# Four graph layers on one core: the last pass as a ring walk, the fronts moved ahead, a longer ring in the first attention pass

## The chip, the cores and the metric
One NeuronCore of one Trainium2 chip. The metric is device time in microseconds (us) of a whole run; the kernel before took 5873.08 us (median of 3 runs, 5872.82 to 5876.18).

## The reference, cut to what matters
A graph of 6250 nodes with 128 features and 100,000 edges, sorted by destination. Four layers, each on `h = relu(layernorm(x))`, each added to `x`:

```python
# layer 0: two GraphSAGE convolutions (mean of the sources' rows, two 128x128 products), elu, log_softmax
# layer 1: attention with 4 heads over the edges and a loop per node, batch norm, 128-512-128 feed-forward, batch norm
# layer 2: attention with 2 heads of 64, prelu
# layer 3:
for r in range(4):
    hr = x_src @ weight[r] + bias[r]          # x_src = h[src]
    msg = where(rel == r, hr, msg)
agg = segment_max(msg, dst); agg = 0 for nodes without edges
x = x + h @ weight[4] + bias[4] + agg
```

Destinations are 6250 u^2 with u uniform, so low nodes have most of the edges.

## The kernel before
Nodes lie as 49 tiles of 128 (NT), in 7 groups of 7 tiles (NG). Edges are padded to 100,352: 784 tiles of 128 (ET). `x` and `h` stay in SBUF. Every layer has a projection (`project`), which normalises the nodes of a group on VectorE and ScalarE (the front), transposes and multiplies on TensorE and writes a table to DRAM, and then a pass over the edges, in which GpSimd gathers the table's rows by edge, 128 rows an instruction.

**Walks.** The two GraphSAGE passes and the second attention pass walk a ring: GpSimd fills slots of 7 tiles (896 edges, GE; 112 groups, GN), and the other engines go through 160 steps (SN), one for each pair of a group and a block of 128 nodes that it touches, with 14 matmul instructions a step that select and add up by products with a one-hot matrix (`add_up`, L1194). `walk_steps` (L880) lays the body of a step out for each engine. The first attention pass does the same with groups of 512 edges, 196 of them in 248 steps, and a ring of QR = 17 groups at the start of `arena`.

**The last pass** is the only one left that doesn't walk. `edge_pass` (defined at L397, called at L2880) goes over 196 chunks of 512 edges. GpSimd gathers four tiles (L422) into one of four slots, with indices that ScalarE copied to `slot` (L514). TensorE transposes the chunk (L495), so that features lie on partitions and edges along them; VectorE scans it (L471): the running maximum, broken by a mask (`cut_row`, loaded by SP, L433) where the destination changes. TensorE transposes it back (L505), ScalarE copies it out of PSUM (L525) and stores all 512 rows to `scan_rows` in DRAM (L531). When all is stored, `gather_results` (L557) has GpSimd gather the row of each node's last edge, 49 times 128 rows, VectorE adds each group of seven to `x` (L2890), and SP stores `out`.

**Projections.** In `project` (L585) VectorE makes front(0) and front(1), then for each group i, where start rows are scattered, waits for the product, copies it (post) and makes front(i+2). GpSimd scatters each group's start rows by seven indirect DMAs (L620), behind the post. In the `by_tile` form TensorE multiplies tile by tile into four PSUM banks, with the transposes of the next group (L650) before tile 4; ScalarE copies the transposed group (L691) and each tile's product (L699). Posts are at L1501 (projection 1), L2405 (2) and L2871 (the y projection of the last layer, L2874).

The passes' starts in the trace: GraphSAGE 58 and 1080 us, first attention pass 2184, projection 2 3552, second attention pass 3664, y projection 4704, last pass 4816.

Of the kernel before, what the change touches and what calls it, by code (L numbers as in the profile page):

```python
# [8 lines left out]
I32 = mybir.dt.int32  # L9
# [4 lines left out]
P = 128  # L14
# [3 lines left out]
NG = 7  # L18
# [10 lines left out]
CHUNKS = ET // CT  # L29
ITERS = CHUNKS // NB  # L30
# [32 lines left out]
QR = 17  # L63
# [61 lines left out]
def build(nc, a, out):  # L125
    assert NT % NG == 0 and ET % CT == 0 and CHUNKS % NB == 0
    groups = NT // NG
    with ExitStack() as ctx:
# [19 lines left out]
        scan_rows = dram("scan_rows", [EP + P, D])  # L148
# [5 lines left out]
        x = sb("x", [P, NT, D])  # L154
        h = sb("h", [P, NT, D])
        arena = sb("arena", [P, 14336])
# [10 lines left out]
        block_col = sb("block_col", [P, 2])  # L167
        last_dst = sb("last_dst", [GN, 1], I32)
# [10 lines left out]
        y_idx = sb("y_idx", [P, ET + (NB + 1) * CT], I32)  # L179
        last_idx = sb("last_idx", [P, NT], I32)  # L180
        start_idx = sb("start_idx", [P, NT], I32)
        slot = sb("slot", [P, NB, CT], I32)
# [62 lines left out]
        group_rows = [count(f"group_rows{b}") for b in range(2)]  # L245
        group_here = count("group_here")
        own_loaded = [count(f"own_loaded{b}") for b in range(2)]
# [4 lines left out]
        gathered = [count(f"gathered{c}") for c in range(NB)]  # L252
        idx_staged = count("idx_staged")
        hot_made = [count(f"hot_made{a}", 2 * LQ) for a in range(2)]
        lo_apart = count("lo_apart")
        numbers_loaded = [count(f"numbers_loaded{b}") for b in range(2)]
        picked = count("picked", NB)
        summed = count("summed", NB)
        chunk_weighted = count("chunk_weighted")
# [18 lines left out]
        own_kept = count("own_kept")  # L278
        own_product = count("own_product")
# [40 lines left out]
        chunk_turned = count("chunk_turned", NB)  # L320
        chunk_scanned = count("chunk_scanned", NB)
        chunk_back = count("chunk_back", 2)
        chunk_copied = count("chunk_copied", 2)
        written = [count(f"written{b}", 16) for b in range(2)]
        mask_loaded = [count(f"mask_loaded{c}") for c in range(NB)]
# [62 lines left out]
        def laps(engine, first, body, n=NB, times=ITERS):  # L388

            first()  # L390
            with engine.Fori(0, times - 1) as i:
                for c in range(n):
                    body(i, c, True)
            for c in range(n):
                body(times - 1, c, c < n - 1)

        def edge_pass(table, width, idx, mask_row, op0, op1, mode="plain"):  # L397

            beside = H1 if mode == "heads" else 0
            target = scan1_rows if beside else scan_rows

            def written_rows(b):
                return out_rows[:, b, 0:CT * (D + beside)].rearrange("p (t d) -> p t d", d=D + beside)

            def rows(c, t):  # L410
                n = (c * CT + t) * width
                return arena[:, n:n + width]

            with nc.Block() as block:
                @block.gpsimd
                def _(pool):
                    with pool.Fori(0, ITERS) as i:
                        for c in range(NB):

                            wait_apart(pool, idx_staged.sem, idx_staged.past(i * NB + c + 1))  # L420
                            for t in range(CT):
# [3 lines left out]
                                ).then_inc(gathered[c].sem, 16)  # L425

                @block.sync
                def _(sp):
                    with sp.Fori(0, ITERS) as i:
                        for c in range(NB):  # L430
                            k = i * NB + c
# [2490 lines left out]
```

## Time and profile before

| | us |
|---|---|
| median of 3 runs | 5873.08 |
| the profiled execution | 5876.16 |
| its span | 5874.4 |
| TensorE matmul busy in it | 3278.1 (56%) |
| VectorE busy | 2906.4 (49%) |
| ScalarE busy | 1827.9 (31%) |
| GpSimd busy | 3903.4 (66%) |

Busy time of GpSimd is that of its gathers alone; the 0.3 us between two gathers isn't in it. A page line of the costliest groups gives the line of the kernel, engine, operation, tiles written and read, the count, then busy time, mean ns of one, and idle time of the engine just before them with what ended it.

### The profile page before, as it was taken

The page shows a single profiled execution, that of the slowest core. Times are in us where ns is not written, and L with a number is a line of the kernel's source. Part 1 is how long each engine was busy: PE and PEld are TensorE (multiplying, and loading weights), DVE is VectorE, ACT ScalarE, POOL GpSimd, SP SyncE. Part 2 cuts the span into 40 slices and gives each one's busy share as a digit, 9 for nine tenths or more (in the row PEclk, how much of TensorE's full clock was granted, in tenths as well). Part 3 has the DMA queues.
Part 4 walks back from the last instruction along what each step waited for, and adds up shares of the span by engine and source line. Part 5 has one row for each costly group of instructions (what it writes and reads, how often), then busy time and mean ns, then how long its engine had stood idle before and what let it go on. Part 6 is the DMA issues. An engine that isn't in the chain of part 4 may idle for free. (4 is left out here: it accounts for less than half of the span.)

```text
span 5874.4 us, 89970 instructions
## 1 busy us (share of the span) xinstructions
PE 3278.1 (56%) x15772; PEld 2756.8 (47%) x15773; DVE 2906.4 (49%) x7625; ACT 1827.9 (31%) x6493; POOL 3903.4 (66%) x4083
## 2 busy tenths in 40 slices
PE   3444555545555525889999894244555563334332
PEld 3444455444555523677777644233445533333331
DVE  4233344434455656788888852344555652222221
ACT  2111111111122213666666653233344441111110
POOL 4777777677777747777776003777777517777776
PEclk9667777766677756999999995566677785555555
DMA  4222222211111112344444211222222134444443
GB/s 122 61 62 63 63 65 66 72 53 52 53 53 52 53 41 78 111 113 117 119 117 113 95 46 31 52 53 54 53 53 52 38 111 130 133 132 130 131 133 107
DMA packets 441899, 474.71 MB, mean 81 GB/s; under 512 B 131954, under 2 KB 337214, under 8 KB 441695
## 3 DMA queue, kind: packets, MB, share of 16 engines
q0 software_dynamic: 130464, 264.37, 17.1%
q1 hardware_dynamic: 184116, 146.31, 8.3%
q10 hardware_dynamic: 127227, 63.09, 3.6%
q14 instruction: 69, 0.57, 0.0%
q8 instruction: 23, 0.38, 0.0%
HBM read 315.46 MB, written 157.97 MB: 81 GB/s over the span
## 5 line engine op out<-in xcount | busy, mean ns | idle before, releaser
L1194 PE MATMUL pa<-arena,weighted 128*128 x4480 | 860.0, 367 | 855.8 <-POOLq L913 511.2
L1194 PEld LDWEIGHTS pa<-arena,weighted 128*128 128x128 f32 x4480 | 795.4, 273 | 909.4 <-issue 909.2
L422 POOL DMA_INDIRECT arena<-y_tab,slot x784 | 739.8, 944 | 398.7 <-issue 209.4
L1607 POOL DMA_INDIRECT arena<-t_tab,src_idx x784 | 777.5, 992 | 265.7 <-issue 216.0
L919 POOL DMA_INDIRECT arena<-h_tab,src_idx x784 | 742.8, 947 | 308.1 <-issue 221.9
L2490 POOL DMA_INDIRECT arena<-t_tab,src_idx x784 | 753.3, 961 | 244.9 <-issue 224.6
L919 POOL DMA_INDIRECT arena<-sage_tab,src_idx x784 | 739.8, 944 | 262.4 <-issue 216.1
L471 DVE TENSOR_TENSOR_SCAN scan_t<-mask,scan_t,pa 128x512 f32<-128x512 bf16 x196 | 250.9, 1280 | 737.1 <-PE pa L495 737.1
L495 PE MATMUL pa<-ident,arena 128*128 128x128 f32 x784 | 218.3, 434 | 603.9 <-DMA arena<-y_tab,slot 603.9
L495 PEld LDWEIGHTS pa<-ident,arena 128*128 128x128 f32 x784 | 140.1, 217 | 681.9 <-DMA arena<-y_tab,slot 430.8
L2731 PE MATMUL pa<-weighted 128*128 128x130 f32 x2240 | 422.6, 364 | 21.0 <-ACT weighted L2809 11.0
L2731 PEld LDWEIGHTS pa<-weighted 128*128 128x128 f32 x2240 | 392.7, 271 | 34.4 <-issue 19.7
L620 POOL DMA_INDIRECT start_rows<-nodeval,start_idx x98 | 98.5, 1005 | 455.1 <-DVE nodeval L2405 372.6
L1056 DVE TENSOR_TENSOR weighted<-pd,rel 128x896 f32<-128x896 f32 x320 | 348.3, 1089 | 51.8 <-issue 47.2
L1064 DVE SCALAR_TENSOR_TENSOR scan_t<-scan_t,alpha,pa 128x130 f32<-128x130 f32 x320 | 110.5, 345 | 503.7 <-PE pb L1201 326.6
L1963 PE MATMUL pa<-weighted 128*128 128x264 f32 x992 | 321.2, 406 | 55.4 <-ACT weighted L2036 35.9
L1239 ACT COPY out_rows<-pb 128x128 f32<-128x128 f32 x320 | 84.6, 264 | 831.5 <-PE pb L1201 700.5
L2036 ACT ACTIVATE weighted<-arena,weighted 128x128 f32 x992 | 322.3, 390 | 62.1 <-POOLq L1598 47.2
L1963 PE MATMUL pa<-arena,weighted 128*128 128x264 f32 x992 | 306.5, 391 | 50.7 <-DVE arena L1769 38.9
L2809 ACT ACTIVATE weighted<-arena,weighted 128x64 f32 x1280 | 323.0, 335 | 19.8 <-ACT weighted L2803 0.2
L525 ACT COPY out_rows<-pb 128x512 f32<-128x512 f32 x196 | 114.7, 585 | 689.4 <-PE pb L505 689.3
L2036 ACT ACTIVATE arena<-arena 128x128 f32 x992 | 312.8, 389 | 14.9
(522 smaller groups left out, 6559.9 us busy)
## 6 DMA issues: line engine op xcount, KB each, us to landing
gat_tab<-out_rows SPq DMA_DIRECT2D x248, 260.0 KB
scan_rows<-out_rows ACTq DMA_DIRECT2D x196, 256.0 KB, 3.7
arena<-t_tab,src_idx POOLq DMA_INDIRECT x1568
mask<-cut_row SPq DMA_DIRECT2D x196, 128.0 KB, 3.1
arena<-h_tab,src_idx POOLq DMA_INDIRECT x784
arena<-sage_tab,src_idx POOLq DMA_INDIRECT x784
y_tab<-arena SPq DMA_DIRECT2D x49, 256.0 KB, 2.3
arena<-y_tab,slot POOLq DMA_INDIRECT x784, 2.8
```

The costliest lines, as they stand in the source:

```text
L422: nc.gpsimd.indirect_dma_start(out=rows(c, t), out_offset=None, in_=table[:, :], in_offset=bass.IndirectOffsetOnAxis(ap=slot[:, c, t:t + 1 ...
L471: v.tensor_tensor_scan(scan_t[:, b, :], mask[:, c, :], pa[:, b * CE:(b + 1) * CE], scan_t[:, 1 - b, CE - 1:CE], op0, op1).then_inc(chunk_s ...
L495: ins = nc.tensor.transpose(to, rows(s, t), ident[:, :])
L919: nc.gpsimd.indirect_dma_start(out=rows[:, g % RG * GT + t, 0:D], out_offset=None, in_=table[:, :], in_offset=bass.IndirectOffsetOnAxis(ap ...
L1056: v.tensor_tensor(hot[b].rearrange("p (t n) -> p t n", n=P), node_row.unsqueeze(1).broadcast_to([P, GT, P]), at.unsqueeze(2).broadcast_to( ...
L1194: ins = nc.tensor.matmul(pa[:, b * CE:b * CE + RW], hot[b][:, t * P:(t + 1) * P], ring[:, bass.ds(start + t * RW, RW)], start=(t == 0), st ...
L1607: nc.gpsimd.indirect_dma_start(out=rows[:, g % QR * QT + t, :], out_offset=None, in_=t1_tab[:, :], in_offset=bass.IndirectOffsetOnAxis(ap= ...
L1963: nc.tensor.matmul(pa[:, b * CE:b * CE + HALF], one, flow1[b][:, t * YW:t * YW + HALF], start=(t == 0), stop=(t == QT - 1))
L2036: ins = nc.scalar.activation(flow1[b][:, at:at + D], ring1[:, bass.ds(start + t * TW, D)], ACT.Copy, scale=flow1[b][:, t * YW + 2 * D + hd ...
L2490: nc.gpsimd.indirect_dma_start(out=rows[:, g % RB * GT + t, :], out_offset=None, in_=t2_tab[:, :], in_offset=bass.IndirectOffsetOnAxis(ap= ...
L2731: ins = nc.tensor.matmul(pa[:, b * CE:b * CE + BW], hot2[b][:, t * P:(t + 1) * P], flow[b][:, t * BW:(t + 1) * BW], start=(t == 0), stop=( ...
L2809: ins = nc.scalar.activation(flow[b][:, at:at + HD], ring2[:, bass.ds(start + t * BW + hd * HD, HD)], ACT.Copy, scale=flow[b][:, at + HD:a ...
```

## The change
- **The last pass is a walk.** GpSimd gathers y_tab by `y_idx` into a ring of 8 groups of 896 edges and, after group 2, gathers the rows of a new DRAM table `last_rows` (for each edge: the node if the edge is its last one, else nothing that matches). Per step ScalarE copies a group out of the ring (stage), TensorE transposes it (turn), VectorE scans it with a carry from step to step, TensorE transposes it back (back), ScalarE copies it from PSUM (keep_back), VectorE builds the one-hot matrix of last rows, TensorE multiplies (select), VectorE adds the block's 128 rows to `x`, and ScalarE stores them to `out` and issues the load of a mask. `scan_rows`, its 51 MB of stores, the 49 gathers and the final adds are gone, and `last_idx` with them.
- **Fronts.** `front(i + 2)` comes before the wait for the product and the post in all projections. The `by_tile` form has two PSUM banks instead of four, and turns and keeps the next group before the tiles of this one.
- **Ring of 28.** QR = 28: the first attention pass's ring lies over `arena` and over `x`, which is spilled to `x_tab` in projection 1 and loaded again in the feed-forward block.
- Some memsets and semaphores that nothing needs now are gone.

```diff
-QR = 17
+QR = 28
-        x = sb("x", [P, NT, D])
-        arena = sb("arena", [P, 14336])
+        wide = sb("wide", [P, 14336 + NT * D])
+        arena = wide[:, 0:14336]
+        x = wide[:, 14336:14336 + NT * D].rearrange("p (j d) -> p j d", d=D)
 ...  project(), VectorE, TensorE, ScalarE
                     def step(i, b, left):
-                        if left > 1 and starts is None:
+                        if left > 1:
                             front(dve, i + 2)
                         dve.wait_ge(group_product.sem, group_product.past(i + 1))
                         post(dve, i, b)
-                        if left > 1 and starts is not None:
-                            front(dve, i + 2)
 ...
-                                if t == 4 and left > 0:
-                                    turn(i + 1)
-                                pe.wait_ge(tile_out.sem, tile_out.by_last_lap(i * NG + (max(t, 1) if t < 3 else max(t - 1, 2))))
-                                to = banks[t % 4][:, 0:n]
+                                pe.wait_ge(tile_out.sem, tile_out.by_last_lap(i * NG + (t + 1 if t > 1 else 2 - t)))
+                                to = pb[:, t % 2 * CE:t % 2 * CE + n]
 ...
-                        if left > 0 and by_tile is None:
+                        if left > 0:
                             turn(i + 1)
 ...
-                        if left > 0 and by_tile is None:
+                        if left > 0:
                             keep(i + 1, 1 - b)
 ...  projection 1, store_rows
+                sp.dma_start(x_tab[i * NG * P:(i + 1) * NG * P, :].rearrange("(j p) d -> p j d", p=P), x[:, i * NG:(i + 1) * NG, :]
+                             ).then_inc(stored.sem, 16)
-            sp.wait_ge(stored.sem, stored.past(32 * groups))
+            sp.wait_ge(stored.sem, stored.past(48 * groups))
 ...
-        ring1 = arena[:, 0:QR * QT * TW]
+        ring1 = wide[:, 0:QR * QT * TW]
 ...  feed-forward block
+            @block.sync
+            def _(sp):
+                sp.dma_start(x, x_tab.rearrange("(j p) d -> p j d", p=P)).then_inc(x_here.sem, 16)
 ...
+                dve.wait_ge(x_here.sem, x_here.past(16))
                 norm_again(0)
 ...  last pass
-        edge_pass(y_tab, D, y_idx, cut_row, ALU.add, ALU.max)
+                for g in range(GN):
+                    if g >= RG:
+                        pool.wait_ge(group_freed.sem, group_freed.past(g - RG + 1))
+                    for t in range(GT):
+                        nc.gpsimd.indirect_dma_start(
+                            out=edge_rows[:, g % RG * GT + t, 0:D], out_offset=None, in_=y_tab[:, :],
+                            in_offset=bass.IndirectOffsetOnAxis(ap=y_idx[:, g * GT + t:g * GT + t + 1], axis=0)
+                        ).then_inc(group_gathered[g % RG].sem, 16)
+                    if g == LAP:
+                        pool.wait_ge(stored.sem, stored.past(16))
+                        for k in range(2):
+                            nc.gpsimd.indirect_dma_start(out=rel_rows[k], out_offset=None, in_=last_rows[:, :],
+                                                         in_offset=bass.IndirectOffsetOnAxis(ap=group_col[:, k:k + 1], axis=0)
+                                                         ).then_inc(table_rows.sem, 16)
 ...  VectorE
+                def scan(s, b):
+                    after(dve, edge_turned, s + 1)
+                    after(dve, mask_loaded[b], (s - b) * 8 + 16)
+                    after(dve, edge_back, s - 1)
+                    after(dve, carry_ready, s)
+                    v.tensor_tensor_scan(run_t[b], mask_t[b], turned_ps[b], carry_t[b], ALU.add, ALU.max).then_inc(edge_scanned.sem, 1)
 ...
+                def body(i, b):
+                    if inside(i):
+                        scan(i, b)
+                        build(i, b)
+                    if inside(i - 2):
+                        add(i - 2, b)
 ...  TensorE
+                def turn(s, b):
+                    after(pe, edge_staged, s + 1)
+                    after(pe, edge_scanned, s - 1)
+                    for t in range(GT):
+                        ins = nc.tensor.transpose(turned_ps[b][:, t * P:(t + 1) * P], staged_t[b][:, t * P:(t + 1) * P], ident[:, :])
+                    ins.then_inc(edge_turned.sem, 1)
+                def back(s, b):
+                    after(pe, edge_scanned, s + 1)
+                    after(pe, edge_kept, s)
+                    for t in range(GT):
+                        ins = nc.tensor.transpose(back_ps[:, t * P:(t + 1) * P], run_t[b][:, t * P:(t + 1) * P], ident[:, :])
+                    ins.then_inc(edge_back.sem, 1)
+                def select(s, b):
+                    after(pe, edge_kept, s + 1)
+                    after(pe, hot_built, s + 1)
+                    after(pe, block_added, s - 1)
+                    for t in range(GT):
+                        ins = nc.tensor.matmul(last_ps[b], hot[b][:, t * P:(t + 1) * P], kept_t[b][:, t * P:(t + 1) * P],
+                                               start=(t == 0), stop=(t == GT - 1))
+                    ins.then_inc(block_summed.sem, 1)
+                def body(i, b):
+                    if inside(i + 1):
+                        turn(i + 1, 1 - b)
+                    if inside(i - 1):
+                        select(i - 1, 1 - b)
+                    if inside(i):
+                        back(i, b)
 ...  ScalarE
+                def stage_group(s, b, start, need):
+                    after(act, edge_turned, s - 1)
+                    wait_apart(act, group_landed.sem, group_landed.past(need))
+                    nc.scalar.copy(staged_t[b].rearrange("p (t d) -> p t d", d=D),
+                                   ring[:, bass.ds(start, GT * RW)].rearrange("p (t w) -> p t w", w=RW)[:, :, 0:D]
+                                   ).then_inc(edge_staged.sem, 1)
+                def keep_back(s, b):
+                    after(act, edge_back, s + 1)
+                    after(act, block_summed, s - 1)
+                    nc.scalar.copy(kept_t[b], back_ps).then_inc(edge_kept.sem, 1)
+                def store(s, b, j):
+                    after(act, block_added, s + 1)
+                    act.dma_start(out[bass.ds(j * P, P), :], x[:, bass.ds(j, 1), :].rearrange("p j d -> p (j d)")
+                                  ).then_inc(block_stored.sem, 16)
+                def body(i, b):
+                    if inside(i):
+                        keep_back(i, b)
+                    if inside(i - 2):
+                        store(i - 2, b, j)
+                    if inside(i) and inside(i + 2):
+                        stage_group(i + 2, b, start, need)
+                        load_mask(i + 2, b, need)
```

## Rows read from the trace of the kernel before

**Rows 1.** The span in 40 slices: busy tenths of GpSimd.
```profile
POOL 4777777677777747777776003777777517777776
```
**Rows 2.** The costliest groups, whole span (columns as told above).
```profile
L1194 PE MATMUL pa<-arena,weighted 128*128 x4480 | 860.0, 367 | 855.8 <-POOLq L913 511.2
...
L422 POOL DMA_INDIRECT arena<-y_tab,slot x784 | 739.8, 944 | 398.7 <-issue 209.4
...
L1056 DVE TENSOR_TENSOR weighted<-pd,rel 128x896 f32<-128x896 f32 x320 | 348.3, 1089 | 51.8 <-issue 47.2
```
**Rows 3.** Windows: length, busy PE, PEld, DVE, ACT, POOL, clock, DMA share, GB/s.
```profile
158.00:358.00 200.00, 93.80 (x442) 87.20 (x442) 59.46 (x182) 22.25 (x78) 151.24 (x161) 0.64 0.22 61
...
758.00:958.00 200.00, 113.73 (x663) 104.33 (x661) 87.58 (x272) 33.06 (x116) 151.03 (x161) 0.79 0.23 65
4656.00:4816.00 160.00, 111.17 (x516) 72.86 (x515) 96.22 (x276) 79.73 (x220) 0.02 (x1) 0.86 0.28 81
...
5216.00:5416.00 200.00, 78.71 (x320) 62.76 (x320) 51.20 (x40) 31.13 (x80) 151.25 (x161) 0.50 0.47 131
```
**Rows 4.** Timeline of a chunk of the last pass: start, duration, engine, line, what.
```profile
5299.22 1.06 PE L505 MATMUL pb<-ident,scan_t 128*128 128x128 f32 x4
5299.47 1.28 DVE L471 TENSOR_TENSOR_SCAN scan_t<-mask,scan_t,pa 128x512 f32<-128x512 bf16 x1 [5.28 <-PE pa L495]
...
5300.40 0.58 ACT L525 COPY out_rows<-pb 128x512 f32<-128x512 f32 x1 [5.29 <-PE pb L505]
...
5301.16 0.38 ACTq L531 DMA_DIRECT2D scan_rows<-out_rows  x1
...
5301.67 0.19 ACT L514 COPY slot<-y_idx 128x4 int32 x1 [0.69 <-ACT out_rows L525]
```
**Rows 5.** Timeline of TensorE: selects of pass 0, transposes of projection 2 and y projection.
```profile
918.28 3.19 PE L1194 MATMUL pa<-arena,weighted 128*128 x14 [2.89 <-POOLq L913]
...
921.65 1.73 PE L1194 MATMUL pa<-arena,weighted 128*128 x14
...
3564.78 1.73 PE L650 MATMUL pa<-ident,weighted 128*128 128x128 f32 x7
...
4795.20 0.93 PE L650 MATMUL pa<-ident,weighted 128*128 128x128 f32 x7
```
**Rows 6.** Timeline of ScalarE in projection 2.
```profile
3566.62 0.91 ACT L691 COPY weighted<-pa 128x896 f32<-128x896 f32 x1 [1.52 <-PE pa L650]
```
**Rows 7.** Timeline of the last pass's start and of GpSimd at its end.
```profile
4815.98 0.94 POOL L422 DMA_INDIRECT arena<-y_tab,slot  x1 [160.09 <-ACT slot L514]
...
4822.20 1.11 PE L495 MATMUL pa<-ident,arena 128*128 128x128 f32 x4 [10.59 <-DMA arena<-y_tab,slot]
...
5793.44 0.94 POOL L422 DMA_INDIRECT arena<-y_tab,slot  x1 [0.30 <-issue]
5806.08 0.94 POOL L557 DMA_INDIRECT arena<-scan_rows,last_idx  x1 [11.70 <-PEq L2881]
```
**Rows 8.** Waits in projection 1 (2079:2185): waiting <- awaited: us, times, longest.
```profile
POOL start_rows L620 <- DVE nodeval L1501: 56.3, 6, 40.9
```
**Rows 9.** Waits in projection 2 (3552:3660).
```profile
POOL start_rows L620 <- DVE nodeval L2405: 372.6, 6, 346.2
```
**Rows 10.** Waits in the y projection (4704:4816).
```profile
PE pb L665 <- ACT arena L699: 10.7, 5, 3.9
```
**Rows 11.** Timeline of TensorE at the end of the feed-forward block.
```profile
3539.05 3.91 PE L2378 MATMUL pa<-ident,arena 128*128 128x128 f32 x16 [3.93 <-ACT arena L2329]
3543.16 0.66 PE L2378 MATMUL pa<-ident,arena 128*128 128x128 f32 x4 [0.19 <-ACT arena L2329]
```
**Rows 12.** First attention pass: waits (3000:3260), and a window (columns as in rows 3).
```profile
POOL arena L1607 <- DVE arena L1769: 9.3, 4, 3.7
POOL arena L1607 <- ACT weighted L2036: 8.1, 7, 2.4
...
3051.00:3091.00 40.00, 37.51 (x173) 30.45 (x172) 35.92 (x90) 28.03 (x103) 29.39 (x30) 1.00 0.41 117
```

More of the change, by code:

```diff
@@ L250, in build @@
         sums_ready = count("sums_ready")
[L252 to L259, printed above, removed]
+        iota_made = count("iota_made")
         table_in = count("table_in")
@@ L583, in group_steps, with project @@
                 step(i, i % 2, min(groups - 1 - i, 2))
-        def project(ns, front, by_tile, by_group, post, begin=None, scalar_front=None, scalar_post=None, gathers=None, store=None,
+        def project(ns, front, by_tile, by_group, post, begin=None, scalar_front=None, scalar_post=None, store=None,
                     buffers=None, starts=None):
             turns = (pa, pd)
-            banks = (pb[:, 0:CE], pb[:, CE:2 * CE], pd[:, 0:CE], pd[:, CE:2 * CE])
             def uses(buf):
@@ L608, in project @@
             with nc.Block() as block:
-                if gathers is not None:
-                    @block.gpsimd
-                    def _(pool):
-                        gathers(pool)
                 if starts is not None:
@@ L748, in project @@
                     tile_stored[buf].base += 16 * uses(buf) * groups
-            if gathers is not None:
-                results_gathered()
             if starts is not None:
@@ new lines, in body, with _, tables, relative @@
+                def body(i, b):
[4 more added lines that the diff above has]
+                        add(i - 2, b)
+                tables()
+                relative()
+                walk_steps(dve, body)
+            @block.tensor
+            def _(pe):
+                def tables():
+                    pe.wait_ge(table_in.sem, table_in.past(1))
+                    nc.tensor.matmul(pa[:, 0:SN], ones[0:1, :], on_row, start=True, stop=True).then_inc(table_on.sem, 1)
+                def relative():
+                    tail = SN - P
+                    pe.wait_ge(table_in.sem, table_in.past(2))
+                    for j in range(GT):
+                        to = (pa, pb)[j // 4][:, j % 4 * 2 * P:(j % 4 + 1) * 2 * P]
+                        nc.tensor.transpose(to[:, 0:P], rel_rows[0][:, j * P:(j + 1) * P], ident[:, :])
+                        ins = nc.tensor.transpose(to[:, P:SN], rel_rows[1][0:tail, j * P:(j + 1) * P], ident[0:tail, 0:tail])
+                    ins.then_inc(table_on.sem, 1)
+                    pe.wait_ge(table_in.sem, table_in.past(3))
+                def turn(s, b):
[25 more added lines that the diff above has]
+                        back(i, b)
+                tables()
+                relative()
+                walk_steps(pe, body)
```

366 lines of the change are left out of this document (145 added, 221 removed).

## The prediction, made before the changed kernel ran
> **What bounds the kernel now.** First the slices of the span [rows 1]: the four graph passes over 784 tiles of 128 edges fill most of it, and in all but the first attention pass the busiest engine is GpSimd, at 0.7 or more. Then the groups by cost [rows 2]: a gather of 128 rows keeps GpSimd 944 ns, and the timeline puts 0.30 us between two [rows 7], so 784 gathers are 784 x 1.247 = 978 us, whatever the others do. Then the windows [rows 3]: in the last pass TensorE is busy 78.7 of 200 us, all at the lower clock (0.50 granted), VectorE 51, ScalarE 31. That pass runs from the first gather at 4816.0 to the last at 5794.4, drains for 11.7 us, and GpSimd then issues 49 gathers of last rows from 5806.1 on [rows 7], 61 us of them at 1.247; the span ends at 5874.4. The last pass is thus 1058.4 us of issue-bound GpSimd: 978 + 12 + 61 + 7. The profiled execution took 5876.16 us, 3.1 above the median; I sum against it and take 3 off at the end.
>
> **Last pass, what goes.** The drain and the 49 late gathers (80 us from 5794.4 on), 196 stores of 256 KB, and ScalarE's index copies, which cost GpSimd nothing before (189.4 us of waits, of which one of 160.1 is the y projection itself [rows 2, 7]). DMA was not the limit: a 0.47 share in this pass [rows 3].
>
> **Last pass, what comes.** 112 groups of 896 edges are walked in 160 steps, because a group that crosses a border of 128 nodes is taken again for the next block. GpSimd still needs 7 x 1.247 = 8.73 us a group, but each step now has a chain of its own. For step i, TensorE's order is turn(i+1), select(i-1), back(i); ScalarE's is keep_back(i), store(i-2), stage(i+2), mask load. keep_back(i) waits for back(i). turn(i+2), TensorE's next work, waits for stage(i+2), which stands behind keep_back(i) and the store in ScalarE's queue. So ScalarE and TensorE take turns: while ScalarE copies, TensorE has nothing that is free to run, since turn(i+2) heads its queue and select(i) and back(i+1) stand behind it. Two buffers don't help, since both orders are fixed.
>
> ScalarE's share of a step: TensorE's end to the copy 0.12 (5300.28 to 5300.40), the gap of a copy, a DMA issue and the next operation 0.69 [rows 4], two copies of 128x896 at 0.91 each [rows 6], and 0.11 back to TensorE, taken like the 0.12: 2.75, with rounding 2.8 us. (The second copy reads the ring and not PSUM; no row has that shape, bounds 0.8 to 1.2.) TensorE's share is 7 transposes, 14 matmul instructions of a select, 7 transposes. At the lower clock they show 1.73, 3.19 to 3.40 and 1.73, at the higher 0.93, 1.73 and 0.93 [rows 5]; less the overlap of an end with the next start, I take 6.37 and 3.34. Hence 9.17 us a step at 1.2 GHz and 6.14 at 2.4 GHz. VectorE's own work is a 896-wide scan of 2.24 (1.28 x 896/512 [rows 4]), a one-hot build of 1.09 [rows 2], two narrow operations and a 128x128 add, under 1.3 together: 4.6, beside TensorE and less than either.
>
> Which clock? In the two GraphSAGE passes, which also work in bursts (TensorE 94 to 114 busy of 200 us), the granted clock averages 0.64 to 0.80, and in the y projection, 111 of 160 busy, 0.86 [rows 3]. The select at 918.28, behind a pause of 2.89 us, runs at the lower clock, and the next one, at 921.65 and right behind the first, at the higher [rows 5]: unbroken work brings the clock up, pauses lose it. A step here is 6.37 us unbroken when slow, which should bring the clock up, and then 2.8 us idle against 3.34 busy, which should lose it again. So a mix. The select costs 860.0/320 = 2.69 us on average over those passes [rows 2], 57% of the way from 1.73 to 3.40; the same here gives 2.8 + 3.34 + 0.57 x 3.03 = 7.9, the midpoint of both ends 7.65. I take 7.7.
>
> Of the 14 + 14 instructions of a step half are transposes. At 3539 sixteen transposes took 3.91 us, 0.24 each, and directly behind them four took 0.66 [rows 11]: transposes alone brought the higher clock. The Trainium skill ("TensorE: Matmul & The Clock Gate", Part 4: PE-mode transpose) says the opposite, that transposes don't count as busy for the clock. By that rule the pass would fall towards the case at 1.2 GHz below; by the row it doesn't.
>
> Start: the gathers of last rows stand behind 21 ring gathers, 28 us, their landing and the relative table take about 12 more: 40 us from the pass's start. (Before, TensorE began 6 us in.) End: back, keep, select, add and a store, about 15 us. The stage is 40 + 160 x 7.7 + 15 = 1287 against 1058.4: **+229 us**. GpSimd is held back by the ring of eight; it has four groups in store at the start, and 7.7 x (steps per group) passes 8.73 soon, so the chain decides nearly throughout. Every 0.1 us a step is 16 us. Break-even, with the other edits, is 6.4 us a step.
>
> **Fronts first.** Projection 1: GpSimd waits for post 56.3 us, 40.9 the first time [rows 8], so 15.4 later: its seven scatters take 7 x 1.285 = 9.0 us and posts come every 12.4. With front(i+2) ahead of the post, scatters run back to back; the first post comes up to 2.5 us later (a front is 7.0 us, 4.85 of which was waited). -13 (0 to -15). Projection 2: 372.6 - 346.2 = 26.4 [rows 9] go by the same reasoning; ScalarE's normalising, which waits for VectorE's front behind the post, kept back the product copies; now that front is early. Left are a first post some 3.4 later, for turn(1) and keep(1) now lie before the products, and perhaps 1 us a group: -16 (+5 to -23). In the y projection the front was ahead already; two product banks instead of four: each tile's product waits for the copy two before. Those waits were 10.7 us [rows 10]; +3 (0 to +8).
>
> **Ring of 28.** In the first attention pass GpSimd is held back by the ring only late: from 3000 to 3260 its waits for the ring are 9.3 and 8.1 us [rows 12], and TensorE is full there at the higher clock (37.5 of 40 us [rows 12]). Gathers that come earlier find TensorE full: 0 (0 to -5; -18 if every wait counted). The spill of x, seven stores of 448 KB on SP's queue in projection 1, hides behind the scatters (0 to +3), its reload behind some 90 us of the feed-forward block. The removed memsets, the cum work and the load of scan_rows are short and in the start: -1 at most.
>
> **Sum.** 5876 + 229 - 13 - 16 + 3 = 6079; less 3: **6076 us**.
>
> **Rivals.**
> 1. The clock stays up, or ScalarE's turn is shorter than I think, so that GpSimd's issue is the bound for half of the pass. At 6.14 a step the first 54 groups go at 8.73 = 471 us, the other 95 steps at 6.14 = 583, with some 16 us of start and end that neither hides 1070: +12 - 26 = 5859 against the median. If the chain is not serial at all, the pass is 978 + 40 + 15 = 1033: 5822. Faster; it decides from 6.4 us a step down. For it: 6.37 us unbroken; 54% busy at the high clock is more than the SAGE passes have. Against: they average 0.64 to 0.80 and lose the clock in pauses of this length. 0.15.
> 2. Clock at 1.2 GHz throughout, as the last pass has now: 40 + 1467 + 15 = 1522, 6311. For it: 0.50 in every window now; against: now only 8 transposes, 2.2 us, come at a time [rows 4]. 0.06.
> 3. The mix is better, with the higher clock for three quarters of the steps: 6.9 us, a stage of 1159, 5948. Part of the main case.
> 4. The fronts' gain doesn't come: +29 on any of these; the ring's 18 us do: -18. Neither turns the sign of the main case.
>
> **Numbers.** Main case 0.75 (steps of 6.6 to 8.5 us: 5900 to 6205), rival 1 0.15, rival 2 0.06, in between near 6.4 0.04. I call less than 0.2%, 12 us, no change, about what can be measured here. Faster 0.16, same 0.03, slower 0.81. Range 5900 to 6210.
>
> **What would show it.** Right: keep_back, store, stage back to back on ScalarE with TensorE idle 2.7 to 2.9 us each step, its wait named as the stage copy; GpSimd waiting for the ring; granted clock 0.6 to 0.85; projection 1 and 2 shorter by 13 and 16. Wrong: GpSimd without waits from 4790 on, TensorE idle in other places, or clock 1.00 or 0.50 throughout.

## The result and the profile after

The changed kernel took 5949.23 us (median of 4 runs, 5945.21 to 5953.10) against 5872.95 for the kernel before (4 runs): ratio 1.0129, interval 1.0112 to 1.0147, 76 us slower. Forecast was 6076, 203 us slower: direction and place are right, the size is 127 us too large.

The page of the changed kernel: slices of the span, and groups (columns as in [rows 2]).

```profile
PE   3445455545555536889999783444555656667776
...
POOL 4777777677777667777773007777777067777772
...
PEclk9667787766777758999999985667677877777777
...
L2704 POOL DMA_INDIRECT wide<-y_tab,y_idx x784 | 807.8, 1030 | 412.0 <-issue 224.6
...
L2842 PE MATMUL pd<-wide,weighted 128*128 128x128 f32 x2240 | 447.8, 383 | 2.0 <-ACT wide L2874 2.0
...
L2874 ACT COPY wide<-pc 128x896 f32<-128x896 f32 x160 | 144.8, 905 | 812.6 <-PE pc L2834 802.5
```

In the last quarter GpSimd is no longer alone: TensorE is at 0.6 to 0.7 and the clock at 0.7, where it was 0.5. And a gather of the last pass takes 1030 ns on average, not the 944 of [rows 2].

The starts of the passes, as the first and last gather of each (count: min/median/max ns, first to last start):

```profile
L1395 POOL DMA_INDIRECT wide<-t_tab,src_idx x784: 940/944/2402, 2174.2 to 3194.8; - x196
L2283 POOL DMA_INDIRECT wide<-t_tab,src_idx x784: 940/944/2572, 3637.0 to 4628.4; - x196
L2704 POOL DMA_INDIRECT wide<-y_tab,y_idx x784: 938/944/1847, 4790.0 to 5850.6; - x196
```

Before they were 2184.4, 3664.0 and 4816.0 us. So the changed kernel is 10.2 us ahead after projection 1, 27.0 after projection 2 and 26.0 at the start of the last pass. From there to the end of the span it needs 5951.3 - 4790.0 = 1161.3 us against 1058.4: +103. Everything that was lost, and everything that I mis-sized (I had 1287), is in this stage. Its last gather starts at 5850.6, 100 us before the end: the steps lag far behind the gathers.

Its windows (columns as in [rows 3]), from the first keep copy on:

```profile
4838.00:5195.00 357.00, 228.99 (x1321) 217.18 (x1320) 186.85 (x239) 86.42 (x96) 274.11 (x273) 0.77 0.32 89
5195.00:5795.00 600.00, 423.25 (x2492) 401.76 (x2492) 346.66 (x445) 158.20 (x178) 463.58 (x441) 0.78 0.35 92
```

VectorE has five operations a step, so the first stretch holds 48 steps of 7.5 us, the second 89 of 6.75 us. Of the 88 intervals between keep copies in the second stretch 74 are 6.9 us, 11 are 5.25 and three are longer. One of the 74 in the timeline:

```profile
5638.91 0.93 PE L2834 MATMUL pc<-ident,weighted 128*128 128x128 f32 x7
...
5639.95 0.91 ACT L2874 COPY wide<-pc 128x896 f32<-128x896 f32 x1 [5.11 <-PE pc L2834]
...
5640.14 0.37 ACTq L2878 DMA_DIRECT2D out<-wide  x1
...
5640.79 0.94 ACT L2863 COPY wide<-wide 128x896 f32 x1
5641.05 0.34 ACTq L2869 DMA_DIRECT2D mask<-cut_row  x1
...
5641.78 1.46 PE L2827 MATMUL pb<-ident,wide 128*128 128x128 f32 x7 [1.95 <-ACT wide L2863]
...
5643.03 2.94 PE L2842 MATMUL pd<-wide,weighted 128*128 128x128 f32 x14
...
5645.80 0.93 PE L2834 MATMUL pc<-ident,weighted 128*128 128x128 f32 x7
```

The chain is there: back, keep copy, stage copy, turn, select, back; TensorE idles while ScalarE copies, and idle is named as the stage copy. But it idles 1.95 us and not 2.75: the store's DMA issue (5640.14) lies under the keep copy, and the stage copy starts the moment that copy ends. Back (0.93) runs at the higher clock, the select (2.94) partly, the turn (1.46) begins at the lower. In the 11 short steps, with the same pause, turn, select and back take 0.98, 1.73 and 0.93. So the mean of 6.75 is no mixture of steps at the one clock and steps at the other: in nearly every step the clock falls and comes back.

The waits of the last pass (waiting <- awaited: us, times, longest):

```profile
ACT wide L2874 <- PE pc L2834: 802.5, 158, 28.5
DVE weighted L2774 <- DMA mask<-cut_row: 325.9, 156, 5.5
...
PE pa L2827 <- ACT wide L2863: 173.1, 79, 5.1
PE pb L2827 <- ACT wide L2863: 168.9, 77, 6.6
...
ACT wide L2863 <- POOLq L2698: 59.8, 23, 13.9
...
POOL wide L2704 <- SPq L2726: 13.9, 4, 5.4
```

A second candidate for the bound stands here, VectorE's waits for the mask (326 us). ScalarE waits 60 us for groups that haven't landed, nearly all in the first third: there GpSimd's supply sets the pace. GpSimd waits for a free slot only four times.

### The profile page after: what moved, and what is told of

The parts are those of the page before. It is cut to its first block and busy times, and to the rows that moved or that the text cites. A ratio compares the mean times of both kernels' runs of the same rounds, so it can differ in the third digit from the quotient of the medians.

```text
span 5951.3 us, 98897 instructions
## 1 busy us (share of the span) xinstructions
PE 3655.1 (61%) x18699; PEld 3175.5 (53%) x18700; DVE 3277.6 (55%) x8233; ACT 1960.4 (33%) x6416; POOL 3930.8 (66%) x4036
## 5 line engine op out<-in xcount | busy, mean ns | idle before, releaser
L991 PE MATMUL pa<-wide,weighted 128*128 x4480 | 851.9, 364 | 866.4 <-POOLq L710 516.6
L991 PEld LDWEIGHTS pa<-wide,weighted 128*128 128x128 f32 x4480 | 787.0, 270 | 920.0 <-issue 919.9
L2704 POOL DMA_INDIRECT wide<-y_tab,y_idx x784 | 807.8, 1030 | 412.0 <-issue 224.6
L716 POOL DMA_INDIRECT wide<-h_tab,src_idx x784 | 742.2, 947 | 306.4 <-issue 222.1
L1395 POOL DMA_INDIRECT wide<-t_tab,src_idx x784 | 778.8, 993 | 246.6 <-issue 221.9
L2283 POOL DMA_INDIRECT wide<-t_tab,src_idx x784 | 753.7, 961 | 244.9 <-issue 223.1
L716 POOL DMA_INDIRECT wide<-sage_tab,src_idx x784 | 739.7, 943 | 262.3 <-issue 216.1
L2842 PE MATMUL pd<-wide,weighted 128*128 128x128 f32 x2240 | 447.8, 383 | 2.0 <-ACT wide L2874 2.0
L2524 PE MATMUL pa<-weighted 128*128 128x130 f32 x2240 | 424.3, 366 | 22.1 <-ACT weighted L2602 13.9
L2842 PEld LDWEIGHTS pd<-wide,weighted 128*128 128x128 f32 x2240 | 432.9, 296 | 2.5 <-ACT wide L2874 2.5
L1824 ACT ACTIVATE weighted<-wide,weighted 128x128 f32 x992 | 322.3, 390 | 66.5 <-POOLq L1386 49.0
L2602 ACT ACTIVATE weighted<-wide,weighted 128x64 f32 x1280 | 323.0, 335 | 19.7
```

What stands on the lines that cost most here:

```text
L716: nc.gpsimd.indirect_dma_start(out=rows[:, g % RG * GT + t, 0:D], out_offset=None, in_=table[:, :], in_offset=bass.IndirectOffsetOnAxis(ap ...
L991: ins = nc.tensor.matmul(pa[:, b * CE:b * CE + RW], hot[b][:, t * P:(t + 1) * P], ring[:, bass.ds(start + t * RW, RW)], start=(t == 0), st ...
L1395: nc.gpsimd.indirect_dma_start(out=rows[:, g % QR * QT + t, :], out_offset=None, in_=t1_tab[:, :], in_offset=bass.IndirectOffsetOnAxis(ap= ...
L1824: ins = nc.scalar.activation(flow1[b][:, at:at + D], ring1[:, bass.ds(start + t * TW, D)], ACT.Copy, scale=flow1[b][:, t * YW + 2 * D + hd ...
L2283: nc.gpsimd.indirect_dma_start(out=rows[:, g % RB * GT + t, :], out_offset=None, in_=t2_tab[:, :], in_offset=bass.IndirectOffsetOnAxis(ap= ...
L2524: ins = nc.tensor.matmul(pa[:, b * CE:b * CE + BW], hot2[b][:, t * P:(t + 1) * P], flow[b][:, t * BW:(t + 1) * BW], start=(t == 0), stop=( ...
```

## The experiments

Theory A: the step is set by the chain of ScalarE and TensorE, and the long gathers come from the one-hot build, whose two inputs are both in SBUF (in the other passes the row of node numbers lies in PSUM). Rival B: the waits for the mask set the step. Rival C: the DMA load makes the gathers long. Theory D, added later: a longer pause is partly given back by the clock.

Step times below are those between the starts of two keep copies from 5195 to 5795 us. Runs are compared with the kernel before on their own chip.

**A first and a second series on disturbed chips.** In these the kernel before took 7382 and 7500 us. Pauses stand between the steps of the last pass, with nothing in the profile to name a cause: of the changed kernel's 159 intervals between keep copies 39 are over 12 us. The engines don't all stand still at once. In the changed kernel ScalarE was idle for more than 7 us 38 times from 6450 us on (516 us in all), and GpSimd started 312 gathers in those stretches; all engines together were idle for 4 us at most at a time, in any of the eight runs. The waits there have a releaser that stands in no wait of the changed kernel on the quiet chip (`waiting <- awaited: us, times, longest`):

```profile
ACT out_rows L1036 <- remote: 809.1, 159, 67.2
ACT wide L2874 <- remote: 634.4, 43, 79.8
```

Their times tell nothing of the change: changed kernel 1.047 of before, stage first 1.031 and 1.027, row in PSUM 1.046 and 1.048, both 1.040 and 1.040, one longer turn 1.052. The medians of the steps over the whole pass tell little more: 7.04 us (changed), 6.09 (stage first, both times), 5.99 (both edits, both times), 7.56 (longer turn), but 6.97 and 7.44 for the same kernel with the row in PSUM on the one and the other chip. What was expected of the first series:

> The changed kernel with one edit: in each step of the last pass ScalarE makes the stage copy of step i+2 and its mask load before it keeps step i's rows, not behind. Theory A (ScalarE and TensorE take turns in one chain): TensorE finds turn(i+2) ready at back(i)'s end, its idle time falls from 1.95 us a step to under 0.5, the clock stays up, and GpSimd is the bound: 784 gathers at the 1.030 us that they take there plus 0.30, and 45 us of start and end, 1088 us for the pass, 5878 us in all (5860 to 5890). Rival B (VectorE's waits for the mask, 326 us, set the step): the step stays 6.9 us, 5949. Rival C (the clock alone): a step below 5 us only if the granted clock goes above 0.9, else unchanged.

> The changed kernel with the row of node numbers, which the one-hot build of the last pass reads, kept in PSUM (as in the other passes) and not in SBUF. Theory A (a build that reads two operands from SBUF holds up GpSimd's gathers): the gathers go from 1030 to 944-950 ns, GpSimd's 68 us come back while it is the bound, some half of the pass; then the chain of 6.9 us a step takes over: 5949 - 35 = 5914 (5890 to 5930). Rival (the gathers are long because of the DMA load of stores and masks): mean of a gather stays near 1030, time unchanged.

> Both edits: stage before keep, and the row of node numbers in PSUM. Theory A: the last pass is 784 x 1.247 = 978 us of gathers and 40 us of start and end, from 4790: 5808 + 2 = 5810 us in all (5795 to 5825), faster than the kernel before by some 60 us. Rival B: as e2, no faster than 5900. A third possibility: VectorE's 4.6 us a step becomes the bound of the last third, where a group has up to 1.9 steps (8.73 / 1.9 = 4.6): 5830 to 5850.

> The changed kernel with an extra copy of 128x768 (about 0.8 us) on ScalarE ahead of each keep copy of the last pass; its result isn't used. This puts TensorE's idle time a step at the 2.75 us on which the prediction rested, in place of 1.95. Theory A: the step becomes 7.4 to 8.1 us by the mix of clocks that the prediction took (7.7), and the pass some 130 us longer: 6080 (6030 to 6140). If the clock doesn't answer to the longer pause, the step grows by 0.8 only, where the chain binds: 6040 to 6060. Rival B (the mask sets the step): under 20 us, 5950 to 5970.

and of the second:

> The changed kernel, unaltered, as a control beside the three that follow. The kernel before took 7382 us in the first series of experiments against 5873 when the change was timed, with pauses on all engines that the profiles don't attribute, so absolute times are only compared within a series. On a chip like the first one: 5949 us against 5873, ratio 1.013.

> The stage copy ahead of the keep copy, again. Theory A (one chain of ScalarE and TensorE): on a chip without the unattributed pauses 5878 us (5860 to 5890), 70 less than the changed kernel; TensorE's idle time in a step under 0.5 us. Rival B (waits for the mask): as the changed kernel.

> The row of node numbers in PSUM, again. Theory A: gathers of 944 to 950 ns for 1030 (the first series showed 944), time 35 us under the changed kernel (20 to 60). Rival (DMA load makes the gathers long): no change in either.

> Both edits, again. Theory A: 5810 us (5795 to 5825), faster than the kernel before by 60. If VectorE's 4.6 us a step binds at the end: 5830 to 5850.

The four edits were run again on quiet chips, below (the kernel before: 5871 to 5881).

**Stage first.** The order of ScalarE's work in a step:

```diff
+                    if inside(i) and inside(i + 2):
+                        stage_group(i + 2, b, start, need)
+                        load_mask(i + 2, b, need)
                     if inside(i):
                         keep_back(i, b)
                     if inside(i - 2):
                         store(i - 2, b, j)
-                    if inside(i) and inside(i + 2):
-                        stage_group(i + 2, b, start, need)
-                        load_mask(i + 2, b, need)
```

> The changed kernel with the stage copy ahead of the keep copy, alone. Theory A: GpSimd becomes the bound with its gathers still long: both edits together gave 5793, and the long gathers cost up to 68 us over the pass: 5830 to 5861. If the chain were not the cause: 5949.

5853.08 us, ratio 0.9954 (0.9937 to 0.9970): 96 us under the changed kernel by the medians, 103 by the two ratios. With the mask load moved along, this edit alone doesn't tell the stage copy from the mask; that load by itself brings nothing (mask earlier, below), so the order of the copies, the chain, is the cause. The first series had expected 5860 to 5890 of it, with gathers of 1030 ns. A quarter of the steps now take 3.84 us or less. GpSimd is the bound: it never waits for a slot, ScalarE waits for its groups, and its gathers are still at 1011 ns:

```profile
L2704 POOL DMA_INDIRECT wide<-y_tab,y_idx x784 | 792.4, 1011 | 400.8 <-issue 230.4
...
ACT wide L2863 <- POOLq L2698: 544.4, 101, 14.0
```

**The row in PSUM.** The build reads a copy of the row behind the turned columns, in the bank of the same step; so turn(i+2) also waits for build(i).

```diff
+                    for ps in (pa, pb):
+                        ins = v.tensor_copy(ps[:, GE:GE + P], iota_f[:, 1:P + 1])
...
-                                    iota_f[:, 1:P + 1].unsqueeze(1).broadcast_to([P, GT, P]),
+                                    (pa, pb)[b][:, GE:GE + P].unsqueeze(1).broadcast_to([P, GT, P]),
...
-                    after(pe, edge_scanned, s - 1)
+                    after(pe, hot_built, s - 1)
```

> The changed kernel with the row of node numbers in PSUM, alone. Theory A: the gathers go to 944 ns, but the chain binds in the second half: 5900 to 5930, 20 to 50 under the changed kernel. If long gathers cost nothing while the chain binds everywhere: 5949.

5952.50 us, ratio 1.0123 (1.0106 to 1.0140): no gain. Theory A's 5900 to 5930 missed; 5949, for long gathers that cost nothing, was near. The gathers did go to 944 ns, with the loads and stores of the changed kernel all in place, which is against rival C:

```profile
L2704 POOL DMA_INDIRECT wide<-y_tab,y_idx x784 | 740.0, 944 | 474.5 <-issue 226.8
```

GpSimd spent it on waiting for slots, 80.6 us for 13.9:

```profile
POOL wide L2704 <- SPq L2726: 80.6, 23, 5.5
```

The median step was 6.96 us for 6.89, with a pause of TensorE of 2.02 for 1.95; the added wait for the build may be in that, and over 160 steps it is some 11 us. In the first third ScalarE's waits for groups fell from 55.7 to 40.5 us. So the edit may give and take about the same. In the changed kernel the long gathers cost, as an estimate from these waits, at most some 15 us, and no difference can be measured.

**Both.**

> Stage ahead of keep and the row of node numbers in PSUM, for the third time, since both series before ran on chips on which even the kernel before was 1500 to 1600 us slower. Theory A, on a chip without these pauses: 5810 us (5795 to 5825), 60 less than the kernel before; in a step TensorE idle under 0.5 us, gathers of 944 to 950 ns. If VectorE's 4.6 us a step binds at the end: 5830 to 5850. Rival B (waits for the mask): 5900 or more.

5793.07 us, ratio 0.9854 (0.9837 to 0.9872): 86 us faster than the kernel before and 156 faster than the changed one, the best version, and 2 us below the range expected. TensorE in a step, and the window 5395 to 5595:

```profile
5589.09 1.82 PE L2846 MATMUL pd<-wide,weighted 128*128 128x128 f32 x14 [0.39 <-ACT wide L2878]
5590.75 0.93 PE L2838 MATMUL pc<-ident,weighted 128*128 128x128 f32 x7
...
5395.00:5595.00 200.00, 144.06 (x1034) 134.74 (x1035) 142.84 (x185) 67.79 (x75) 151.23 (x161) 0.87 0.40 107
```

Idle is 0.39 us, the select's wait for the keep copy, beside which the turn now runs; GpSimd issues 161 gathers in 200 us, as before the change [rows 3]. The pass takes 5790.4 - 4790.2 = 1000 us, 978 of them gathers. Against stage first alone, the row in PSUM is worth 60 us, now that GpSimd is the bound.

**Mask earlier.** The mask load of step i+2 ahead of the keep copy of step i.

```diff
+                    if inside(i) and inside(i + 2):
+                        load_mask(i + 2, b, need)
                     if inside(i):
                         keep_back(i, b)
```

> The changed kernel with the mask load of step i+2 issued ahead of the keep copy of step i, 2 us and more earlier. Rival B (VectorE's waits for the mask, 326 us, set the step): 5949 - 100 or more, below 5850. Theory A (VectorE is beside the chain): the waits for the mask go, the time stays within 10 us of 5949.

5963.47 us, ratio 1.0139 (1.0122 to 1.0156): not faster, and within 10 us of the changed kernel by the two ratios (1.0129), though not by the medians, for the kernel before took 5881 on this chip. VectorE's waits for the mask are no longer among the longest; it waits for the turn in their place:

```profile
DVE weighted L2774 <- PE pa L2827: 105.3, 78, 4.1
DVE weighted L2774 <- PE pb L2827: 102.7, 79, 4.9
```

Rival B falls: a wait of 326 us in total bound nothing.

**The row in SBUF where it was in PSUM.** The kernel before, with one line of the GraphSAGE passes changed:

```diff
-                                        node_row.unsqueeze(1).broadcast_to([P, GT, P]),
+                                        iota_f[:, 0:P].unsqueeze(1).broadcast_to([P, GT, P]),
```

> The kernel before, with one edit in the two GraphSAGE passes: their one-hot builds read the row of node numbers from SBUF and not from PSUM (320 builds). It tests whether such a build holds up GpSimd where nothing else is changed. Both passes are bound by the gathers. Theory A: their mean goes from 944-947 ns to 1010-1030, and the kernel takes 2 x 60 = 120 us more: 5995 (5970 to 6015). Rival (the long gathers of the changed last pass come from its DMA load): no change, 5875.

5992.56 us, ratio 1.0202 (1.0185 to 1.0219): 121 us slower, 120 were expected. Groups of the page and a stretch of the timeline:

```profile
L919 POOL DMA_INDIRECT arena<-h_tab,src_idx x784 | 792.7, 1011 | 308.1 <-issue 231.3
L919 POOL DMA_INDIRECT arena<-sage_tab,src_idx x784 | 813.6, 1038 | 262.2 <-issue 234.3
...
405.66 1.08 DVE L1056 TENSOR_TENSOR weighted<-iota_f,rel 128x896 f32<-128x896 f32 x1
406.31 1.25 POOL L919 DMA_INDIRECT arena<-h_tab,src_idx  x1 [0.30 <-issue]
407.86 0.94 POOL L919 DMA_INDIRECT arena<-h_tab,src_idx  x1 [0.31 <-DMA arena<-h_tab,src_idx]
```

The means were 947 and 944. A gather that starts while the build runs (405.66 to 406.74) takes longer, the next doesn't. So it is throughout: in the second pass the 145 gathers that start under a build take 1.45 us on average, 1.86 at most, and the 639 others 0.94; in the changed kernel's last pass 134 take 1.45 and 650 take 0.94. The edit moves no data by DMA, so rival C falls. The Trainium skill ("SBUF — State Buffer", Who interferes with whom) has this rule: a VectorE operation with both inputs in SBUF keeps out a GpSimd operation that reads SBUF, and the later one waits for the other's end. The traces agree: the gather reads its indices from SBUF, the cost goes with the operand's place, and 135 of those 145 gathers end 0.8 us after the build's end, wherever in it they began. A build that starts under a gather takes 1.09 us as any other; so of the two only the gather is seen to wait. The prediction lacked this term; in the changed kernel as it is, it was nearly hidden, and it is 60 us as soon as the chain is mended.

**One and two longer turns.** Copies that nothing uses, ahead of the keep copy: one of them puts TensorE's pause near the one that I had predicted with.

```diff
+                    nc.scalar.copy(arena[:, 6 * GE:6 * GE + 6 * P], back_ps[:, 0:6 * P])
                     nc.scalar.copy(kept_t[b], back_ps).then_inc(edge_kept.sem, 1)
```

> An extra copy of 128x768 on ScalarE ahead of each keep copy: TensorE's idle time a step 2.75 us, as the prediction had it, for 1.94. Theory A, that the pause was the mis-sized term: the step becomes 7.4 to 8.1 us and the time comes near the 6076 predicted (6030 to 6140). On the chips with long pauses of all engines the median step was 7.57 against 7.04 for the changed kernel, which would give only +0.5 x 160 = 85 over 5949: 6030. If the step grows by the 0.8 alone: 6060 to 6075.

> The changed kernel with two extra copies of 128x768 on ScalarE ahead of each keep copy: TensorE's idle time a step about 3.3 us, after 1.94 in the changed kernel (step 6.9, 5949 us) and 2.61 with one such copy (step 7.03, 5966 us). If the step answered to the pause by the clock's mix with a constant share of the lower clock, both would have grown by the copies; they didn't. Theory D (the clock gives back what a longer pause takes, up to a point): between the bounds at 2.4 GHz (6.6) and 1.2 GHz (9.6), if the point is not yet reached 7.0 to 7.3 and 5970 to 6010; if it is, 7.8 to 8.5 and 6090 to 6200.

One: 5965.61 us, ratio 1.0145 (1.0128 to 1.0162). Two: 6073.96 us, ratio 1.0342 (1.0325 to 1.0360). Windows 5395 to 5595 us of the changed kernel, with one copy more, with two:

```profile
5395.00:5595.00 200.00, 141.72 (x831) 134.50 (x831) 116.17 (x150) 53.36 (x60) 155.50 (x147) 0.77 0.35 92
```
```profile
5395.00:5595.00 200.00, 124.02 (x819) 116.91 (x817) 115.58 (x149) 71.12 (x88) 153.07 (x155) 0.85 0.35 93
```
```profile
5395.00:5595.00 200.00, 114.46 (x726) 108.30 (x724) 101.26 (x130) 81.34 (x104) 119.27 (x120) 0.82 0.29 78
```

| | pause, us | fastest steps | how many | median step | mean step | granted clock |
|---|---|---|---|---|---|---|
| changed | 1.95 | 5.25 | 11 of 88 | 6.89 | 6.75 | 0.77 |
| one copy | 2.61 | 5.92 | 35 of 87 | 7.25 | 6.82 | 0.85 |
| two copies | 3.31 | 6.62 | 35 of 77 | 8.08 | 7.76 | 0.82 |

The fastest steps are those wholly at 2.4 GHz: they grow by 0.67 and 0.70 us, so the copies do lie in the chain. The mean grows by 0.07 for the first and by 0.94 for the second. With 3.03 us between a step at the one and at the other clock, the share of TensorE's work at the lower one is (6.75 - 5.25) / 3.03 = 0.50, then 0.30, then 0.38. The first copy's cost was given back by the clock; what I had expected of one copy (6030 to 6140) missed. Theory D fits in kind, and my two cases for two copies both missed: the step came between them. (In the first third, to 5195 us, the step is 7.54 us with and without one copy, since gathers set the pace there.)

The order of the steps is not chance. With one copy the same five follow each other through the whole stretch, 7.25, 5.92, 7.49, 5.92 and 7.56 us; with two, 8.1, once or twice 6.62, and 9.3; in the changed kernel about twenty of 6.89 and then three of 5.25. Two turns with one copy, behind the same pause:

```profile
5508.30 1.75 PE L2827 MATMUL pb<-ident,wide 128*128 128x128 f32 x7 [2.61 <-ACT wide L2863]
5509.85 2.34 PE L2842 MATMUL pd<-wide,weighted 128*128 128x128 f32 x14
...
5515.56 0.98 PE L2827 MATMUL pa<-ident,wide 128*128 128x128 f32 x7 [2.61 <-ACT wide L2863]
5516.38 1.73 PE L2842 MATMUL pd<-wide,weighted 128*128 128x128 f32 x14
```

So the pause right before doesn't decide alone: one turn starts at the lower clock, the next at the higher. Which step meets which clock, and so why the share moves as it does, stays open.

**The ring of the first attention pass.** QR = 17 in the changed kernel.

> The changed kernel with the ring of the first attention pass at 17 groups again (x is still spilled and loaded). By the prediction the ring brings 0, at most 5 us: 5949 to 5954. By the rival that every wait for the ring counted: 5967.

5951.87 us, ratio 1.0137 (1.0120 to 1.0154), against 1.0129 with 28: no difference. With 28 groups the pass's last gather starts at 3194.8 us for 3214.1, 19 us earlier, and the next pass's first gather at 3637.0 for 3636.4.

**The projections alone.** The kernel before with the change to `project`, first as it is in the change, then with four banks and only the front moved:

```diff
-                        if left > 1 and starts is None:
+                        if left > 1:
                             front(dve, i + 2)
                         dve.wait_ge(group_product.sem, group_product.past(i + 1))
                         post(dve, i, b)
-                        if left > 1 and starts is not None:
-                            front(dve, i + 2)
```

> The kernel before with the change to the projections alone (front(i+2) before the post, two product banks, next group turned before the tiles); last pass and ring as before. By the prediction: -13 in projection 1, -16 in projection 2, +3 in the y projection: 26 under the kernel before (5847 for 5873). By the rival that fronts bring nothing: 5873.

> The kernel before with front(i+2) ahead of the post in the two projections that scatter start rows, the four product banks and the order of the transposes as before. By the prediction -13 and -16, and without the +3 of two banks in the y projection: 5844 (5835 to 5855), a little under the kernel with two banks (5852). If the two-bank order (next group turned first) were what brings the gain in projection 2: 5860.

5852.49 us, ratio 0.9957 (0.9942 to 0.9972), and 5845.69 us, 0.9956 (0.9939 to 0.9972): 25 us each against their own chips' kernel before; 26 and 29 were expected. The front's place is the gain; the banks make no difference that can be told from zero. 1.0129 / 0.9957 = 1.0173 is left for walk and ring, 102 us, as the stage showed.

## Why the prediction was right, and where it was wrong

The term of the sum that was mis-sized is the step of the last pass: 7.7 us forecast, 6.95 measured as the mean of the 159 intervals, and 0.75 x 160 = 120 of the 127 us. It was put together from a pause of 2.8 us and a constant share of the lower clock; both were wrong, as the second and fourth points below say.

- *What bounds, and the chain.* Right. keep copy, store, stage copy and turn stand one behind the other as said, and the reordering that breaks the chain brings back 96 us.
- *"The gap of a copy, a DMA issue and the next operation 0.69".* This step failed. In [rows 4] the DMA issue waited for its own copy (the kernel waits for `chunk_copied` ahead of it), and the next copy's start fell behind that; the 0.69 was a wait, and I took it for the price of issuing. The new store has data that are long ready, and costs the chain nothing. The pause is 1.95 us and not 2.75.
- *TensorE's 3.34 and 6.37 us.* 3.34 was right: the fastest steps are 5.25 = 1.95 + 3.30. 6.37 wasn't reached: no step of that stretch is wholly at the lower clock, and the slowest with two copies have 9.35 - 3.31 = 6.04. VectorE's 4.6 us were too many: its five operations take 2.08 + 0.21 + 0.22 + 1.09 + 0.29 = 3.9, and in the best version many steps last 3.74, TensorE's 3.3 and its wait of 0.39.
- *The mix of clocks, 57% at the lower.* This step failed too. 50% was measured in the changed kernel. With the true pause my own sum gives 1.95 + 3.34 + 0.57 x 3.03 = 7.0 us, and 40 + 160 x 7.0 + 15 = 1175 for a stage that took 1161. By the sum, the pause is thus nearly the whole error. (That it comes out so near is luck: a share of 0.50 for 0.57 takes 34 us off, and the wait for gathers in the first third, 47 steps of 7.54 for 6.89, puts 31 on.) By the experiment it isn't: with a pause of 2.61 the step was 6.82 and not 7.6 or more, so a forecast with the wrong pause would have been nearly right if the share had been. I had carried a share from another pass over as if it were a constant; it moved between 0.30 and 0.50 here as the pause went from 1.95 to 3.31, and by what rule stays open.
- *Start 40 us, end 15.* The first keep copy began 48 us after the first gather, the last 8 us before the span's end: 56 in all, for the 55 taken.
- *GpSimd's supply.* "The chain decides nearly throughout": the first third went at 7.5 us a step with ScalarE waiting for gathers, which I had not. The longer gathers were not foreseen; as the chain stood they cost next to nothing.
- *Fronts.* -13, -16, +3 forecast; -10.2, -16.8, +1.0 measured by the passes' starts. Of the 10.2 the changed kernel had 2.5 already at the start of the second GraphSAGE pass (1077.5 for 1080.0), so projection 1 brought 7.7. In projection 1 GpSimd waits once, for the first post, in projection 2 4.8 us beside the first:

```profile
POOL start_rows L425 <- DVE nodeval L1286: 44.5, 1, 44.5
```
```profile
POOL start_rows L425 <- DVE nodeval L2198: 373.6, 6, 368.8
```

- *Ring.* 0 forecast, 0 measured; the waits of [rows 12] went (ScalarE's to 0.3 us), and nothing came of it; that TensorE was full there fits.
- *Rivals.* The second, 1.2 GHz throughout, fell: the granted clock was 0.77 and 0.78, in a pass half of whose instructions on TensorE are transposes, and in the best version seven of them take 0.93 us. The Trainium skill ("TensorE: Matmul & The Clock Gate", Part 4: PE-mode transpose) has it that they don't count as busy for the clock in the same way. That transposes run at the higher clock this pass shows; whether they bring it up it can't show, for here each turn is followed by a select. Only [rows 11] speak against the sentence there. The first, a clock that stays up, came true only with the chain broken, and then at 5793. Its price for a chain that isn't serial, 1033 us for the pass, adds 40 us of start during which GpSimd in fact gathers on: 1000 were measured. The third, higher clock for three quarters of the steps, named 5948; its number was hit within 1 us by luck: the clock was high for half of the work and not three quarters, and the shorter pause made up for it.

## What to carry to other kernels

When one engine's queue holds both the producer of the next step and the consumer of this one, ask which stands first: two buffers don't help if the order makes the producer wait for this step's end. Swapping two copies was worth 96 us here, and turned a loss of 76 us into a gain. A gap in a timeline is a cost in the new kernel only if what ended it would be there in the new place too; look for what the instruction behind the gap waited for. And keep one operand of a long VectorE operation out of SBUF where GpSimd's gathers are the bound.

## What was not expected of the hardware

- A build of 128x896 with both inputs in SBUF lengthened the gathers that started under it, to 1.45 us for 0.94: 944 to 1038 ns on average over a pass, 121 us for 320 builds, about 0.38 us a build.
- A pause on TensorE that was 0.67 us longer cost 0.07 us a step, as the granted clock went from 0.77 to 0.85; a second one cost 0.94. Steps of the same work and pause took 5.92 to 7.56 us, in an order that repeats.
- On two of the chips ScalarE and TensorE stood still for 7 us and more again and again, while GpSimd mostly gathered on, and the same kernel took 7382 and 7500 us for 5873. The walks lost more there: the best version was 1.040 of the kernel before, where it is 0.985 on a quiet chip. No run shows why.
